# Quantising in 1024-column pieces, and moving the row maxima and the ternary conversion of w_down in a post-LN layer

## The reference

```
def _act_quant(x, bits=8):
    scale = 127 / clip(max(abs(x), axis=-1), EPS)
    return clip(round(x * scale), -127, 127) / scale
def _weight_quant(w):
    s = clip(mean(abs(w)), EPS)
    return clip(round(w / s), -1, 1) * s
h = einsum(_act_quant(x), _weight_quant(w_up))
h = square(relu(h))
out = einsum(_act_quant(h), _weight_quant(w_down))
x = layernorm(x + out)
```

## Time and profile before

| | us |
|---|---|
| three runs | 3419.2, 3550.34, 3546.36 |
| their median | 3546.36 |
| profiled execution, its own time | 3426.36 |
| its span on the slowest core (core 4) | 3424.8 |
| spans of the eight cores | 3391.5 to 3424.8 |
| up front, first ScalarE instruction to last cell | 2464.7 to 2629.1 |
| up loop | 2629.1 to 2875.8 |
| down front | 2879.8 to 3096 |
| down loop | 3096 to 3378.7 |
| tail | 3378.7 to 3424.8 |

### The profile page before, as it was taken

One profiled execution on the slowest core, in us unless ns is written; L12 is line 12 of the kernel. 1 busy time (PEld: TensorE's weight loads), 2 busy tenths in 40 slices (PEclk: granted clock), 3 DMA queues, 4 the chain that ended last, 5 costly groups with the idle time before them and its releaser, 6 DMA issues.

```text
span 3424.8 us, 37469 instructions; the slowest of 8 cores (3391.5 to 3424.8 us)
## 1 busy us (share of the span) xinstructions
PE 2360.9 (69%) x14730; PEld 1454.3 (42%) x14730; DVE 1207.7 (35%) x1553; ACT 645.1 (19%) x1072; POOL 287.4 (8%) x453
## 2 busy tenths in 40 slices
PE   0267677798797887888239999949445886455673
PEld 0122224143352432424038888814223765344563
DVE  0144442322223222223521111154524665754434
ACT  0022220311212112021201111103222213241111
POOL 3100003010110100100010101000000000000000
PEclk9999898798897988888569999959656988667886
DMA  8766554120120211200084747036201342303222
GB/s 125 137 178 179 167 173 68 13 25 6 20 25 1 25 13 13 25 0 1 0 98 51 91 59 99 2 50 138 83 0 49 99 125 75 96 1 98 75 86 111
DMA packets 194594, 229.54 MB, mean 67 GB/s; under 512 B 15091, under 2 KB 162548, under 8 KB 193396
## 3 DMA queue, kind: packets, MB, share of 16 engines
q0 software_dynamic: 134160, 109.10, 20.4%
q1 hardware_dynamic: 59108, 109.66, 10.9%
q10 hardware_dynamic: 1152, 8.39, 0.6%
HBM read 294.23 MB, written 8.39 MB: 88 GB/s over the span
## 4 chain that ended last, share of the span: by engine, by line
PE 57%; DVE 18%; DMA 15%; ACT 4%; issue 3%; POOL 2%; DVEq 1%; ACTq 0%; SPq 0%; POOLq 0%
PE ps_all L743 13%; PE ps_all L1094 8%; PE ps_all L434 7%; PE ps_all L451 7%; PE ps_all L1276 5%; DMA swst<-wdnT 4%; PE ps_all L494 4%; PE ps_all L499 4%; DMA swst<-wupT 4%; DVE denr L560 3%; PE ps_all L955 3%; PE ps_all L516 3%; DVE swpart L309 2%; PE ps_all L571 2%; DVE wdb L1239 2%
## 5 line engine op out<-in xcount | busy, mean ns | idle before, releaser
L743 PE MATMUL ps_all<-membuf,sigT 128*128 128x256 bf16 x4096 | 449.9, 274 | 36.4 <-DMA membuf<-mem 36.4
L325 PE MATMUL ps_all<-xTb,wqb 128*128 128x512 bf16 x1024 | 260.2, 414 | 258.9 <-DMA wqb<-wqT 147.7
L743 PEld LDWEIGHTS ps_all<-membuf,sigT 128*128 128x128 bf16 x4096 | 401.4, 98 | 84.7 <-issue 36.5
L1276 PE MATMUL ps_all<-wdb,rtq 128*128 128x256 bf16 x2048 | 255.8, 293 | 142.5 <-DVE wdb L1239 135.8
L1094 PE MATMUL ps_all<-wub,xqT 128*128 128x256 bf16 x2048 | 263.9, 298 | 51.6 <-DVE wub L1022 38.1
L1276 PEld LDWEIGHTS ps_all<-wdb,rtq 128*128 128x128 bf16 x2048 | 213.7, 105 | 184.5 <-issue 146.2
L325 PEld LDWEIGHTS ps_all<-xTb,wqb 128*128 128x128 bf16 x1024 | 103.2, 104 | 415.4 <-issue 325.5
L1094 PEld LDWEIGHTS ps_all<-wub,xqT 128*128 128x128 bf16 x2048 | 215.0, 106 | 99.0 <-issue 58.3
L434 PE MATMUL ps_all<-xTb,kw 128*128 128x512 bf16 x1024 | 237.7, 397 | 9.6 <-DMA kw<-wkT 9.6
L451 PE MATMUL ps_all<-vw,xTb 128*128 128x256 bf16 x2048 | 224.9, 273 | 0.0
L451 PEld LDWEIGHTS ps_all<-vw,xTb 128*128 128x128 bf16 x2048 | 200.0, 98 | 25.2
(11 more groups left out here) (159 smaller groups left out, 2134.8 us busy)
## 6 DMA issues: line engine op xcount, KB each, us to landing
swst<-wupT SPq DMA_DIRECT2D x64, 512.0 KB, 4.5
swst<-wdnT SPq DMA_DIRECT2D x64, 512.0 KB, 4.7
membuf<-mem POOLq DMA_DIRECT2D x64, 512.0 KB, 18.3
wfs<-wupT POOLq DMA_DIRECT2D x16, 1024.0 KB, 6.5
wfs<-wupT SPq DMA_DIRECT2D x16, 1024.0 KB, 6.1
wfd<-wdnT SPq DMA_DIRECT2D x16, 1024.0 KB, 6.5
wfd<-wdnT POOLq DMA_DIRECT2D x16, 1024.0 KB, 6.7
xTb<-xT POOLq DMA_DIRECT2D x64, 128.0 KB, 9.0
```

The costliest lines, as they stand in the source:

```text
L325: k.emit("tensor", lambda t, oc=oc, lc=lc, dc=dc, bank=bank: t.matmul(ps[bank][:, 0:CH], wqb[:, dc * D + oc * 128: dc * D + (oc + 1) * 128 ...
L743: k.emit("tensor", lambda t, ss=ss, m=m, dc=dc, bank=bank, buf=buf: t.matmul(ps[bank][:, 0:256], sigT[:, dc * OWN + ss * 128: dc * OWN + ( ...
L1276: k.emit("tensor", lambda t, ss=ss, ic=ic, bank=bank, buf=buf: t.matmul(ps[bank][:, 0:256], rtq[:, qbase(ss) + ic * 128: qbase(ss) + ic * ...
```

## The change

It has four parts. (1) In the up front, each row block is quantised in two halves of 1024 columns: each half has its two ScalarE and two VectorE instructions, its eight transposes and its copy, in this order. (2) In the up loop, the eight row maxima of group g are written no longer behind the matmuls of `it` = 4g + 3, but into the next iteration, behind its conversion and its normalisation; those of the last group stand behind the loop. (3) In the down front, each row block is quantised in four quarters of 1024 columns instead of two halves of 2048, `rqtile` now having two halves of its own; the first four steps wait for `last_v[0]`, later ones for the `rqtile` of four steps before. (4) In the down loop, the conversion of weight group `ht` + 1 is written behind cell 2 of group `ht`, and only that of group 2 stays ahead of the loop.

```diff
         for ss in range(8):
-            civ = s_emit(lambda s, ss=ss: s.activation(
-                sciT[:, 0:D], x2[:, ss * D:(ss + 1) * D], AF.Relu,
...
+            for h2 in range(2):
+                step = ss * 2 + h2
+                off = h2 * 1024
+                xoff = ss * D + h2 * 1024
...
+                v_emit(lambda v, off=off: v.scalar_tensor_tensor(
+                    adjb[:, off:off + 1024], scq[:, off:off + 1024], -0.5,
+                    sciT[:, off:off + 1024], ALU.add, ALU.is_gt),
+                    waits=[(sse, scv)])
+                xqv = v_emit(lambda v, off=off: v.scalar_tensor_tensor(
+                    xqtile[:, off:off + 1024], sciT[:, off:off + 1024],
+                    -128.0, adjb[:, off:off + 1024], ALU.add, ALU.add),
+                    waits=[(tmm, tp_hist.get(step - 2, b3_last))])
...
-            for ss in range(8):
-                evac_mark[(it, ss)] = emit_c2_mm(it, ss)
-            up_t[it % 2] = tmm.n
-            if it % 4 == 3:
-                g = it // 4
+            if it % 4 == 0 and it >= 4:
+                g = it // 4 - 1
                 for ss in range(8):
                     v_emit(lambda v, ss=ss, g=g: v.reduce_max(
                         pmax[:, ss * 4 + g: ss * 4 + g + 1],
                         rtq[:, ss * DI + g * 1024: ss * DI + (g + 1) * 1024],
                         AX.X, apply_absolute_value=True),
-                        waits=[(sse, evac_mark[(it, ss)])])
+                        waits=[(sse, evac_mark[(4 * g + 3, ss)])])
+            for ss in range(8):
+                evac_mark[(it, ss)] = emit_c2_mm(it, ss)
+            up_t[it % 2] = tmm.n
+        for ss in range(8):
+            v_emit(lambda v, ss=ss: v.reduce_max(
+                pmax[:, ss * 4 + 3: ss * 4 + 4],
...
         for ss in range(8):
-            for hc in range(2):
-                step = ss * 2 + hc
-                sci_, scq_, adj_ = qset[step % 2]
-                o0 = ss * DI + hc * 2048
+            for qc in range(4):
+                step = ss * 4 + qc
+                sci_, scq_, adj_ = qset[(step % 4) // 2]
+                off = (step % 2) * 1024
+                o0 = ss * DI + qc * 1024
                 wts_ci = [(sdbg, dbg_gate3),
-                          (vve, rq_hist[step - 2] if step >= 2
+                          (vve, rq_hist[step - 4] if step >= 4
                            else last_v[0])]
...
+                rqv = v_emit(lambda v, off=off, sci_=sci_, adj_=adj_: v.scalar_tensor_tensor(
+                    rqtile[:, off:off + 1024], sci_[:, off:off + 1024],
+                    0.0, adj_[:, off:off + 1024], ALU.add, ALU.add),
+                    waits=[(tmm, tp3_done.get(step - 2, b3_last))])
                 rq_hist[step] = rqv
...
+        adv_dn(12)
         for ht in range(2, 8):
-            adv_dn((ht + 1) * 4)
             for ss in range(8):
                 emit_c4_mm(ht, ss)
                 flush_cells(keep=1)
+                if ss == 2 and ht < 7:
+                    adv_dn((ht + 2) * 4)
             dn_t[ht % 2] = tmm.n
```

More of the change, by code:

```diff
@@ L1109, in build_program @@
         evac_mark = {}
-        tp_done = [0] * 8
-        xqv_hist = [0] * 8
+        tp_hist = {}
+        xqv_hist = {}
         for ss in range(8):
-            civ = s_emit(lambda s, ss=ss: s.activation(
-                sciT[:, 0:D], x2[:, ss * D:(ss + 1) * D], AF.Relu,
[L1115 to L1131, removed]
+            for h2 in range(2):
+                step = ss * 2 + h2
+                off = h2 * 1024
+                xoff = ss * D + h2 * 1024
+                scv = None
+                s_emit(lambda s, off=off, xoff=xoff, ss=ss: s.activation(
+                    sciT[:, off:off + 1024], x2[:, xoff:xoff + 1024],
+                    AF.Relu, bias=cq1[:, 8 + ss:9 + ss],
+                    scale=cq1[:, ss:ss + 1]),
+                    waits=[(vve, fin_v), (vve, xqv_hist.get(step - 2, 0))])
+                scv = s_emit(lambda s, off=off, xoff=xoff, ss=ss: s.activation(
+                    scq[:, off:off + 1024], x2[:, xoff:xoff + 1024],
+                    AF.Relu, bias=cq1[:, 8 + ss:9 + ss],
+                    scale=cq1[:, ss:ss + 1]))
+                if h2:
+                    scq_s[ss] = scv
+                v_emit(lambda v, off=off: v.scalar_tensor_tensor(
[6 more added lines that the diff above has]
+                    waits=[(tmm, tp_hist.get(step - 2, b3_last))])
+                xqv_hist[step] = xqv
+                bank = step % 2
@@ L1132, in build_program @@
                 wts = [(vve, xqv)] + bank_w(bank)
                 for j in range(8):
-                    dc = g * 8 + j
+                    dc = h2 * 8 + j
                     k.emit("tensor", lambda t, dc=dc, j=j, bank=bank: t.transpose(
@@ L1139, in build_program @@
                 tpv = tmm.n
-                ev = v_emit(lambda v, ss=ss, g=g, bank=bank: v.tensor_copy(
-                    xqT[:, ss * D + g * 1024: ss * D + (g + 1) * 1024],
+                tp_hist[step] = tpv
+                ev = v_emit(lambda v, ss=ss, h2=h2, bank=bank: v.tensor_copy(
+                    xqT[:, ss * D + h2 * 1024: ss * D + (h2 + 1) * 1024],
                     psb[bank][:, 0:1024]), waits=[(tmm, tpv)])
                 bank_guard[bank] = (vve, ev)
-            tp_done[ss] = tmm.n
             xq_evac[ss] = last_v[0]
@@ L1174, in build_program @@
                         AX.X, apply_absolute_value=True),
-                        waits=[(sse, evac_mark[(it, ss)])])
+                        waits=[(sse, evac_mark[(4 * g + 3, ss)])])
[5 more added lines that the diff above has]
+                pmax[:, ss * 4 + 3: ss * 4 + 4],
+                rtq[:, ss * DI + 3 * 1024: ss * DI + 4 * 1024],
+                AX.X, apply_absolute_value=True),
+                waits=[(sse, evac_mark[(15, ss)])])
         c2_last = tmm.n
@@ L1313, in build_program @@
                            else last_v[0])]
-                s_emit(lambda s, o0=o0, ss=ss, sci_=sci_: s.activation(
-                    sci_[:, 0:2048], rtq[:, o0:o0 + 2048], AF.Square,
+                s_emit(lambda s, o0=o0, off=off, ss=ss, sci_=sci_: s.activation(
+                    sci_[:, off:off + 1024], rtq[:, o0:o0 + 1024], AF.Square,
                     scale=sc3[:, ss:ss + 1]), waits=wts_ci)
-                sqv2 = s_emit(lambda s, o0=o0, ss=ss, scq_=scq_: s.activation(
-                    scq_[:, 0:2048], rtq[:, o0:o0 + 2048], AF.Square,
+                sqv2 = s_emit(lambda s, o0=o0, off=off, ss=ss, scq_=scq_: s.activation(
+                    scq_[:, off:off + 1024], rtq[:, o0:o0 + 1024], AF.Square,
@@ L1319, in build_program @@
                     scale=sc3[:, ss:ss + 1]))
[L1320 to L1326, removed]
@@ L1327, in build_program @@
-                rq_hist[step] = rqv
[L1328 to L1343, removed]
+                v_emit(lambda v, off=off, sci_=sci_, scq_=scq_, adj_=adj_: v.scalar_tensor_tensor(
+                    adj_[:, off:off + 1024], scq_[:, off:off + 1024], -0.5,
+                    sci_[:, off:off + 1024], ALU.add, ALU.is_gt),
+                    waits=[(sse, sqv2)])
@@ new lines, in build_program @@
+                rqv = v_emit(lambda v, off=off, sci_=sci_, adj_=adj_: v.scalar_tensor_tensor(
+                    rqtile[:, off:off + 1024], sci_[:, off:off + 1024],
+                    0.0, adj_[:, off:off + 1024], ALU.add, ALU.add),
+                    waits=[(tmm, tp3_done.get(step - 2, b3_last))])
+                rq_hist[step] = rqv
+                bank = step % 2
+                wts = [(vve, rqv)] + bank_w(bank)
+                for j in range(8):
+                    k.emit("tensor", lambda t, off=off, j=j, bank=bank: t.transpose(
+                        psb[bank][:, j * 128:(j + 1) * 128],
+                        rqtile[:, off + j * 128: off + (j + 1) * 128],
+                        idb[:]),
+                        waits=wts if j == 0 else (),
+                        inc=tmm if j == 7 else None)
@@ L1344, in build_program @@
                 tp3_done[step] = tmm.n
+                ev = v_emit(lambda v, ss=ss, qc=qc, bank=bank: v.tensor_copy(
+                    rtq[:, qbase(ss) + qc * 1024: qbase(ss) + (qc + 1) * 1024],
+                    psb[bank][:, 0:1024]), waits=[(tmm, tp3_done[step])])
+                bank_guard[bank] = (vve, ev)
             rq_done[ss] = last_v[0]
```

## The result

The changed kernel takes 3357.6 us (median of nine runs, 3351.6 to 3391.3). The ratio to the kernel before is 0.983, with a 95% interval of 0.979 to 0.986: 1.7% less, a gain clear of the noise and just under 2%. The forecast was 3364 with a range of 3338 to 3386.

A forecast was written before the change was run, and what follows sets the result against it. TensorE was taken to stand still waiting for VectorE, in both loops and both fronts. The terms -2 - 38 + 27 - 49.6 = -62.6 took 3426.4 to 3364 us; 8 in 10 within 3338 to 3386.

The forecast's parts named there:

- The halved instructions: Both fronts: at 1024 columns `adj` and `rqtile` take 1.225 us, ScalarE's instructions 1.10 (1.13 in the up front).
- Up front: Quantising in halves shortens a row block's chain from 12.04 to 11.77 us, gaining 2 us over 8 blocks.
- Up loop: Conversion ahead of the maxima removes three stalls of 10.1 us and 2.6 of clock loss each; gain 38 us.
- Down front: Quarters bring a second wait for transposes, 1.27 us, in each half; loss of 27 us.
- Down loop: Earlier conversion removes waits of 16.6 us but leaves a new stall of 6.5 per loop; gain 49.6 us.
- first rival, first half: Down loop: the clock survives the 6.5 us stall, so five times 2.1 = 10.5 us go; whole rival 3341, chance 0.12.
- the second half's 12 us: Down front: transposes 3.6 us apart keep full clock, saving about 12 us; same rival, 3341, chance 0.12.
- second: Rival, down front: the quarters cost nothing as finer pieces overlap the engines; 3337 us, chance 0.06.
- third: Rival, down loop: the moved conversion does not overlap and the 49.6 us are lost; 3413 us, chance 0.06.
- fourth: Rival, both fronts: 96 halved VectorE instructions stay at 2.29 us, adding 102; 3466 us, chance 0.02.

The follow-up runs named there:

- e2: Kernel before with only the up loop's row maxima written one iteration later; up loop 199.6 us against 237.0, ratio 0.991.
- e3: Kernel before with only the down front cut into quarters of 1024; down front 242.9 us against 216.1, ratio 1.009.
- e4: Kernel before with only the next group's w_down conversion written behind cell 2; down loop 215.6 us against 263.1, ratio 0.986.
- e6: Changed kernel with each down-front quarter's copy written behind adj and rqtile of the next quarter; down front 210.7 us against 240.5.

## Why the prediction was right

**The halved instructions.** `adj` and `rqtile` of 1024 columns take 1.225 us, exactly the figure taken from the slope of two reductions. ScalarE's were set too low: 1.15 and 1.24, in place of 1.10 and 1.13. By line and shape (busy, mean ns), changed kernel:

```profile
L1338 DVE SCALAR_TENSOR_TENSOR rqtile<-sciT,adjb 128x1024 bf16<-128x1024 int32 x32 | 39.2, 1225 | 3.4
...
L1331 ACT ACTIVATE scq<-rtq,sc 128x1024 f32<-128x1024 bf16 x32 | 36.7, 1148 | 3.0
...
L1123 ACT ACTIVATE scq<-x,cq 128x1024 f32<-128x1024 bf16 x16 | 19.8, 1240 | 1.5
```

**Up front** (-2 forecast). Measured -1.5 in the changed kernel, and -1.6 to -3.3 in kernels that don't have part 1 at all (e2, e3, e4), so the stage's -1.5 confirms nothing. The chain of a block is 12.13 us (2453.48 to 2465.61) where 11.77 was worked out and 12.04 stood before: of the 0.36 too little, 0.22 are ScalarE's two longer halves. The true gain is nothing, this term was mis-sized, and the mechanism, a chain with a second wait for transposes, stands.

**Up loop** (-38). Measured -37.5, and the stage alone in e2 -37.4. All steps came as written: conversion ahead of the maxima, three stalls and their clock loss gone. One term was too small. The conversion for `it` = 5 was to be late by 0.2 us and is late by 0.85, twice. VectorE and TensorE in order of time, changed kernel:

```profile
2658.01 1.22 DVE L1175 TENSOR_REDUCE pmax<-rtq 128x1 f32<-128x1024 bf16 x1 [0.17 <-DVE pmax L1175]
2659.40 1.22 DVE L1175 TENSOR_REDUCE pmax<-rtq 128x1 f32<-128x1024 bf16 x1 [0.17 <-DVE pmax L1175]
2660.86 1.29 DVE L1017 TENSOR_SCALAR tnb<-wfs,thrup 128x2048 bf16<-128x2048 f32 x1 [0.24 <-DVE pmax L1175]
...
2668.78 1.47 PE L1094 MATMUL ps_all<-wub,xqT 128*128 128x256 bf16 x12 [0.85 <-DVE wub L1022]
```

The maxima follow each other in 1.39 us, not 1.32: the gap is 0.17, since each waits for two semaphores, and eight of them make 0.6 us of the 0.65.

**Down front** (+27). Measured +24.4, and alone in e3 +26.8. The cause given, a second wait for the transposes in every half, is confirmed by e6. By row blocks the losses were 4.8, 4.8, 5.8 and five times 1.7 us, where 4.4, 5.5, 5.5 and five times 2.3 stood. Blocks 3 to 7 repeat in 23.97 where the terms gave 24.8 and 24.6 was taken: the second group of transposes always finds the full clock (a wait of 0.86 in place of 1.26), and the first copy starts 9.55 us behind the flush (2961.80 to 2971.35) in place of 10.05, as the two cells ahead of the transposes end after 9.0 and not 9.4. A serial quarter of block 0 takes 7.10 us (7.0 forecast).

**Down loop** (-49.6). Measured -47.9, alone -47.5. The five waits are 32.5 us, 6.5 each, as worked out, and they are where they were said to be. The slow-clock restart after each is 1.5 to 3 us, mean 2.5 rather than 2.1: between two of these waits 256 matmuls take 29.4 to 31.0 us, where 27.9 would be full clock. Behind the first of them the granted clock is 0.50 for 3.9 us and 0.96 over the next 27:

```profile
3120.12 30.97 PE L1289 MATMUL ps_all<-wdb,rtq 128*128 128x256 bf16 x256 [6.51 <-DVE x L1301]
3157.53 29.37 PE L1289 MATMUL ps_all<-wdb,rtq 128*128 128x256 bf16 x256 [6.43 <-DVE x L1301]
```

**The sum.** -62.6 forecast, -62.5 measured in the feed-forward half of the profiled execution. That it agrees to 0.1 us is luck: the down front lost 2.6 less than forecast and the other stages gained 2.6 less. The eight cores' own lengths of this half differ by up to 8 us in one execution, and by the ratio of runs the gain is 59 us (48 to 71). What the prediction had right is each stage's mechanism, and its size within 3 us.

**The rivals.** The clock did not survive the shorter stalls in the down loop (first rival, first half); of the transposes 3.6 us apart, the second group keeps the full clock (granted 1.00, eight in 0.61 us) and the third and fourth do not (0.50, 1.01 us), so of the second half's 12 us about 3 came. The quarters do not come free (second) unless the copies are moved. The conversion overlaps (third). Halved instructions get shorter (fourth). The rule cited from the Trainium skill ("VectorE: DVE Perf Modes", the section on the errata), that pieces of at least 512 elements amortise the fixed cost, holds for the instructions themselves here, 1.225 against half of 2.29; it doesn't say what a piece costs through the waits that it brings, 1.26 us each, and the measurement decides that here.

## What to carry to other kernels

Cutting a tile into smaller pieces only pipelines engines if each engine's instructions are written so that it has something to do while the other works on its piece; written piece after piece, every piece adds one full handover (1.26 us here, +24 us in all), and moving one copy by one piece turned that into a gain. When work is moved beside matmuls, what stands behind it on its engine is the next stall: count how many results the matmuls can produce before they need a buffer that this engine must free, and move the work in pieces that fit between two of those frees. And in a chain over three engines each engine's order is a bound of its own: shifting ScalarE's alone won 50 of 97 us here (170.7 to 121.2, and 73.4 with all shifted) and then showed the next wait.

## What the runs showed of the hardware

- Between two instructions of VectorE, the second not held up otherwise, the gap is 0.10 us if it waits for one semaphore and 0.17 if it waits for two. The maxima show it: 0.10 was assumed, 0.17 measured, while `adj` to `rqtile` stays at 0.10 (2962.92 + 1.23 to 2964.25); the second wait in `rqtile`'s code is not written out, since VectorE has already passed it. It is not the copy ahead, as the prediction had it: a flush behind a copy has one wait and starts after 0.11 (2984.99 + 0.69 to 2985.79), `adj` behind a copy has two and starts after 0.17.
- ScalarE's square with a per-partition scale takes 1.148 us at 1024 and 2.002 at 2048 columns, its relu with a per-partition bias as well 1.240 and 2.092: 0.83 ns for a column in both, and 0.09 us between them. Whether that is the bias or the function isn't shown here.
- TensorE ran the up loop's 1792 matmuls in 199.6 us with the granted clock at 0.99; before, at 0.92, three idle stretches of 10 us each cost another 2.6 at the lower level.
